# Attention scores computed once, in query rows, with the exponentials transposed afterwards

## The chip, the cores and the metric

The kernel runs on one core of a Trainium2 chip. The metric is the device time of one execution in microseconds (us). TensorE (PE) multiplies matrices, and its weight loads are listed apart (PEld); VectorE (DVE) and ScalarE (ACT) read and write both memories, PSUM and SBUF; GpSimd (POOL) works in SBUF alone; SyncE (SP) starts the transfers from and to DRAM. Each engine runs its own list of instructions in order and waits on semaphores. TensorE's granted clock is recorded as a share of 2.4 GHz: 1.00 is 2.4 GHz, 0.50 is 1.2 GHz, and what lies between is a mean over time at either level.

## What is computed

x has 8 batches of 112 queries with 256 features, the context 8 batches of 375 keys. Two layers follow one another; in each there is attention on the context and then a feed-forward part:

```python
x = x + _L0_xattn_ref(_layernorm(x), ctx, ...)       # 16 heads of 16, with biases, no mask
x = x + _L0_ffn_ref(_layernorm(x), ...)              # 8 experts, the best 2 for each token
x = x + _L1_xattn_ref(_layernorm(x), ctx, ..., mask) # 16 heads of 16, no biases, a 112 x 375 mask
x = x + _L1_ffn_ref(_layernorm(x), ...)              # rounded weights and a short convolution
```

The attention, in both layers:

```python
attn = jnp.einsum('bhqd,bhkd->bhqk', qp, kp) * SCALE
attn = jax.nn.softmax(attn, axis=-1)
out = jnp.einsum('bhqk,bhkd->bhqd', attn, vp)
```

The softmax goes over the 375 keys, so it needs a maximum over them for each query and head, exponentials, and their sum. The product with the values contracts over the keys, so the exponentials have to stand with the keys on the partitions for it. Products of full precision are made from a high and a low part of each operand (`product3`: high times high, high times low, low times high).

## The kernel before

The program has five stages: a setup (lines 82 to 108), attention a0, the experts, attention a1 (both from `attention_layer`), and the last feed-forward part. A barrier of all engines stands between stages. The setup loads x and waits for it before the barrier.

In `attention_layer` everything goes batch by batch, with the queries projected for all batches at the start. For one batch, in the order in which the data flow:

- `context` transposes the context (6 transposes into PSUM); ACT writes the high part, DVE the low part. `keys` and `values` project it: 12 matmuls of 376 columns and 18 of 256.
- `spread` copies the keys into a head layout `kst`. Each head pair has rows 0 to 47 and 64 to 111, with high and low parts stacked (48 = 3 x 16 rows), made by 16 matmuls with a selection matrix `sel` and 4 evictions of 752 columns. `stacked` does the same to the queries (`qst`), once for each half of the batches.
- `scores_for_max` computes the scores with the queries on the partitions (two heads to a matmul pair, L695), and `maxima` on DVE takes the maximum of each row (L469 in a0; in a1 the mask is added in the same instruction, L473).
- `parts`, `max_rows` (L703) and `shift` turn the maxima into rows and subtract them from the queries by two more rows of the contraction.
- `scores` computes the scores a second time, now with the keys on the partitions: six units a batch, each of 8 matmuls of 50 rows (L723). In a1 each unit has 4 more matmuls of 448 columns which add the mask (L717). ACT takes the exponential of each unit in one instruction of 896 columns (L343).
- `weigh` multiplies by the values: four groups a batch, each 12 matmuls that write 32 columns of the array (L738; each is recorded twice, so 24). A column of ones gives the sum. `gathered`, `turned` and `output` transpose back, DVE divides, and the output projection and the addition to x follow.

Two PSUM tiles `pair` of 1024 columns are handed around in the order of the list `order`, one tile `s1` holds the scores for the maxima, and `misc` holds the small products in the order of `small`. A unit in a tile waits until the reader of the unit before in the same tile is done. The loop over b interleaves the second scores of batch b, the first scores of b+1, and the context of b+2; the order of the calls in the tensor block is the order on TensorE. GpSimd does nothing in the loop.

## Time and profile before

| | |
|---|---|
| median of 3 runs | 889.59 us (885.14 to 893.82) |
| the profiled execution | 894.33 us, span 892.6 us |
| setup and attention a0 | 0 to 267.7 us of the span |
| first exponential of a0, of a1 | at 76.9 us, at 607.2 us |
| experts | 267.7 to 538.0 us |
| attention a1 | 538.0 to 804.5 us |
| last feed-forward part | 804.5 to 892.6 us |
| busy over the span | PE 669.3 us, DVE 434.3 us, ACT 288.7 us, POOL 47.5 us |

The stage borders are the first instructions after each barrier. Busy time of PE is the union of its matmuls from issue to modelled end, so a group of matmuls that is listed with 0.65 us gives the array to the next group earlier than that: what a group costs in a full row of work is the distance from its start to the start of the next one.

### The profile page before, as it was taken

Reading aid. Unit: us, or ns where it says so; the run is one execution under the profiler, and the core shown is the slowest. Engines: PE = TensorE matmul, PEld = TensorE weight load, DVE = VectorE, ACT = ScalarE, POOL = GpSimd, SP = SyncE. Lnnn points to the kernel's source line nnn. Section 1 sums busy time; section 2 is a strip of 40 time slices with the busy share of each in tenths; the row PEclk is TensorE's granted clock in tenths of the full one; section 3 lists DMA queues with packets and bytes.
Section 4 is the critical chain, followed back from the end, with each engine's and each line's share of the span. In section 5 each row is a group of like instructions: output and inputs, shape, how many; then the busy total and the mean of one; then the engine's idle time right before and its main releaser. Section 6 shows DMA issues by size and latency. Waiting matters only on the chain. (4 is left out here: it accounts for less than half of the span.)

```text
span 892.6 us, 13908 instructions
## 1 busy us (share of the span) xinstructions
PE 669.3 (75%) x5473; PEld 552.5 (62%) x5473; DVE 434.3 (49%) x1204; ACT 288.7 (32%) x505; POOL 47.5 (5%) x59
## 2 busy tenths in 40 slices
PE   0679989898883604999998722879999999982744
PEld 0657777777662604998898721767777777762533
DVE  3556555656613240243221344465555546626895
ACT  1433343444322001332233212324433343334530
POOL 1010000000000042000000071000000000000000
PEclk9988778999756655999999965989999999995888
DMA  5000000000009844455555023000000000000001
GB/s 141 23 17 18 19 11 9 1 1 1 1 2 302 258 182 158 174 179 175 178 177 171 25 82 112 13 18 19 19 19 1 1 1 1 2 2 1 1 0 41
DMA packets 39728, 57.05 MB, mean 64 GB/s; under 512 B 5209, under 2 KB 32881, under 8 KB 39537
## 3 DMA queue, kind: packets, MB, share of 16 engines
q1 hardware_dynamic: 38128, 52.50, 18.3%
q0 software_dynamic: 1536, 3.67, 1.3%
q8 instruction: 44, 0.72, 0.3%
q14 instruction: 20, 0.16, 0.1%
HBM read 47.91 MB, written 8.26 MB: 63 GB/s over the span
## 5 line engine op out<-in xcount | busy, mean ns | idle before, releaser
L343 ACT ACTIVATE a_e<-a_pair 125x896 f32<-125x896 f32 x96 | 88.2, 919 | 145.0 <-PE a_pair L723 143.8
L473 DVE CUSTOM_DVE_ANT_0 a_masked<-a_s,a_mask 112x375 f32<-112x375 f32 x128 | 65.3, 544 | 52.2 <-issue 52.2
L1385 PE MATMUL ex_h<-ex_xg_t,w_s 128*128 128x128 f32 x672 | 80.8, 280 | 0.1
L1133 ACT ACTIVATE ex_h_t<-ex_h,b_e 128x128 f32<-128x128 f32 x168 | 47.9, 369 | 101.4 <-PE ex_h L1385 101.4
L1385 PEld LDWEIGHTS ex_h<-ex_xg_t,w_s 128*128 128x128 f32 x672 | 79.0, 197 | 0.5 <-DVE ex_xg_t L1280 0.5
L1397 PE MATMUL ex_y<-w_s,ex_h_t 128*128 128x256 f32 x336 | 75.8, 379 | 0.0
L469 DVE TENSOR_REDUCE a_mx<-a_s 112x2 f32<-112x750 f32 x64 | 59.9, 936 | 29.2 <-PE a_s L695 28.6
L723 PEld LDWEIGHTS a_pair<-a_q,a_kst 50*125 50x125 f32 x768 | 55.1, 203 | 27.3 <-issue 20.4
L723 PE MATMUL a_pair<-a_q,a_kst 50*125 50x112 f32 x768 | 67.1, 298 | 4.3 <-DVE a_kst L463 4.2
L695 PE MATMUL a_s<-a_kst,a_qst 48*112 48x376 f32 x256 | 54.8, 422 | 19.2 <-DVE a_mx L469 10.8
L1397 PEld LDWEIGHTS ex_y<-w_s,ex_h_t 128*128 128x128 f32 x336 | 62.3, 190 | 7.6
L670 PE MATMUL a_pair<-a_kp,a_sel 128*128 128x376 f32 x256 | 58.3, 352 | 0.9 <-ACT a_kst L327 0.8
L39 PE MATMUL a_pair<-a_ct,a_wr 128*128 128x376 f32 x192 | 48.7, 418 | 12.7 <-DVE a_ct L444 12.7
L1286 DVE TENSOR_TENSOR ex_y_sb<-ex_y,b_all 128x256 f32<-128x256 f32 x21 | 8.9, 425 | 100.2 <-PE ex_y L1397 100.2
L738 PE MATMUL a_av<-a_e,a_v 125*32 125x112 f32 x1536 | 57.4, 293 | 0.0
L717 PE MATMUL a_pair<-ident_r,a_mask_r 112*125 112x448 f32 x192 | 50.5, 384 | 4.6 <-DVE a_kst L463 4.2
L39 PEld LDWEIGHTS a_pair<-a_ct,a_wr 128*128 128x128 f32 x192 | 43.3, 248 | 14.5 <-issue 11.5
L738 PEld LDWEIGHTS a_av<-a_e,a_v 125*32 125x32 f32 x1536 | 41.0, 122 | 12.1 <-issue 10.6
L670 PEld LDWEIGHTS a_pair<-a_kp,a_sel 128*128 128x128 f32 x256 | 41.9, 190 | 7.8 <-issue 6.3
L695 PEld LDWEIGHTS a_s<-a_kst,a_qst 48*112 48x112 f32 x256 | 24.8, 185 | 31.5 <-issue 13.0
L39 PE MATMUL a_misc<-a_wr,a_ct 128*125 128x256 f32 x288 | 42.8, 294 | 1.8 <-ACT a_v L337 1.6
L39 PEld LDWEIGHTS a_misc<-a_wr,a_ct 128*125 128x125 f32 x288 | 36.8, 189 | 7.6 <-issue 7.6
(252 smaller groups left out, 917.4 us busy)
## 6 DMA issues: line engine op xcount, KB each, us to landing
w_s<-in_L_ffn_W SPq DMA_DIRECT2D x21, 1024.0 KB, 5.0
w_all<-in_L_ffn_W SPq DMA_DIRECT2D x8, 1024.0 KB, 12.0
a_ctx<-in_ctx SPq DMA_DIRECT2D x16, 375.0 KB
x_slots<-ex_zeros SPq DMA_DIRECT2D x1, 2688.0 KB, 13.5
ex_xg<-x_slots SPq DMA_DIRECT2D x21, 128.0 KB, 4.8
y_slots<-ex_y_sb SPq DMA_DIRECT2D x21, 128.0 KB, 1.7
b_all<-in_L_ffn_b SPq DMA_DIRECT2D x1, 1024.0 KB
wu<-in_L_ffn_w SPq DMA_DIRECT2D x1, 1024.0 KB, 5.9
```

The costliest lines, as they stand in the source:

```text
L39: ins = nc.tensor.matmul(out, a, b, start=first and k == 0 and n == 0, stop=last and k == len(w) - 1 and n == 2)
L343: a.activation(es[:, c, kc], halves(bank("s2", b, c, kc)[0:KP], 4 * S), ACT.Exp, scale=scale)\
L469: v.reduce_max(mx[:, t], halves(s1[0:S], SK), AX.X).then_inc(max_out, 1)
L473: ins = v.tensor_tensor_reduce(out=masked[:, e], in0=s1[0:S, e * 512:e * 512 + SK], in1=mask_sb[:], scale=1.0, scalar=-3.0e38, op0=ALU.add ...
L670: last = nc.tensor.matmul(bank("ks", b, i)[:, j * 512:j * 512 + SKP], sel[:, 1, part, n], kp[:, part, c], start=part == 0, stop=part == 1)
L695: last = nc.tensor.matmul(s1[0:S, e * 512:e * 512 + SKP], qst[rows, t, columns(b)], kst[rows, b % 3, t], start=True, stop=True)
L717: nc.tensor.matmul(out[0:KP, e * 512:e * 512 + 4 * S], mask_r[:, part, ks], ident_r[0:S, :], start=part == 0, stop=False)
L723: last = nc.tensor.matmul(out[0:KP, e * 512 + n * S:e * 512 + (n + 1) * S], kst[rows, b % 3, t, ks], q2[rows, t], start=mask is None, stop ...
L738: last = nc.tensor.matmul(av[32 * n:32 * n + 32, g * S:(g + 1) * S], vx[:, b % 3, kc, 2 * (4 * c + n) + e], es[:, c, kc, e, n * S:(n + 1) ...
L1133: last = a.activation(h_t[:, i % 2, f], hb[i % 2][:, f * 128:(f + 1) * 128], ACT.Gelu, bias=b1_e[:, i % 2, f:f + 1])
L1385: last = nc.tensor.matmul(hb[i % 2][:, f * 128:(f + 1) * 128], w1_s[:, i % 3, k, f * 128:(f + 1) * 128], xg_t[:, i % 2, k * 128:(k + 1) * ...
L1397: last = nc.tensor.matmul(yb[i % 2][:, 0:D], h_t[:, i % 2, f], w2_s[:, i % 2, f * D:(f + 1) * D], start=f == 0, stop=f == FC - 1)
```

## The change

- The scores are computed once, with the queries on the partitions. A step t covers four heads of one batch (32 steps in a layer). Its 12 matmuls of 376 columns work on 32 rows each, rows 32r to 32r+31 for head r, in three passes (high times high, high times low, low times high); the four heads write four PSUM banks of the one tile `s`. The queries for even and odd heads lie in `qz` with the other head's rows set to zero, so that the keys need no layout of their own: `kst`, `qst`, `sel`, `spread`, `stacked`, `parts`, `max_rows`, the second scores and the mask matmuls go.
- `maxima` takes two heads at a time and then scales the two maxima into the bias of the exponential. `exps` makes one ACTIVATE for each head (112 x 375). In a0 it reads PSUM; in a1 it reads the masked scores, which the maximum instruction now writes to SBUF.
- `turned` transposes the exponentials: three PSUM units a step, each of 4 transposes, copied to `et`: one by ACT and two by DVE in a0, two by ACT and one by DVE in a1.
- PSUM is now `s` (4 banks) and a ring of four single banks in the order of `order`.
- The high and low parts of context, keys and attention output (from batch 1 on for context and keys) are made by GpSimd, two instructions each, from a raw copy that ACT takes out of PSUM. GpSimd also adds the output bias batch by batch, and computes the reciprocal deviation with a power.
- The setup no longer loads x: a0 loads it in two halves among its weights. Biases are loaded as rows and turned by small matmuls. The second half of the queries is normalized, transposed and projected in steps 0 to 4 of the loop.

The core of the diff, indentation reduced; of functions that are rewritten only the new lines stand:

```diff
-    @block.sync
-    def _(sp):
-        sp.dma_start(x_sb[:], x.rearrange("b s d -> s b d")).then_inc(x_in, 16)
-        sp.wait_ge(x_in, 16)
...
     wr = sb(f"{tag}_wr", [128, 2, 4, DC, D], F32R)
-    qst = sb(f"{tag}_qst", [128, HP, T], F32R)
-    kst = sb(f"{tag}_kst", [128, 3, HP, SKP], F32R)
...
+    kp = sb(f"{tag}_kp", [128, 2, 2, DC, SKP], F32R)
...
-    vx = sb(f"{tag}_v", [KP, 3, KC, H, 32])
-    mx = sb(f"{tag}_mx", [S, HP, 2])
...
+    s = pb(f"{tag}_s", (128, 2048))
+    ring = [pb(f"{tag}_ring{i}") for i in range(4)]
...
+    order = [("wt", 1), ("wt", 0)] if transposed else [("bias",)]
+    order += [("ct", 0, 0), ("ct", 0, 1), ("k", 0, 0), ("k", 0, 1), ("xt", 0, 0), ("xt", 0, 1), ("q", 0, 0), ("q", 0, 1)]
+    order += [("wt", 2), ("wt", 3)] if transposed else [("bo",)]
+    order += [("v", 0, 0), ("v", 0, 1)]
+    for t in range(-1, NQ + 4):
+        b, g = divmod(t, 4)
+        step = [("et", t, kc) for kc in range(KC)] + [("av", t - 1)]
+        step = [u for u in step if 0 <= u[1] < NQ]
+        work = [[("v", b + 1, 0)], [("avt", b - 1), ("k", b + 1, 0)], [("ot", b - 1), ("v", b + 1, 1), ("k", b + 1, 1)],
+                [("ct", b + 2, 0), ("ct", b + 2, 1), ("y", b - 1)]][g]
+        order += step + [u for u in work if 0 <= u[1] < B]
+        order += {2: [("xt", 1, 0), ("xt", 1, 1)], 3: [("q", 1, 0)], 4: [("q", 1, 1)]}.get(t, [])
     place = {u: i for i, u in enumerate(order)}
...
+            def load_x(half):
+                bs = slice(4 * half, 4 * half + 4)
+                sp.dma_start(x_sb[:, bs], x_from.rearrange("b s d -> s b d")[:, bs]).then_inc(x_in[half], 16)
+
+            if x_from is not None:
+                load_x(0)
+                sp.dma_start(b_row[:, 0:D], bias_q.rearrange("(o n) -> o n", o=1)).then_inc(b_in, 16)
+                sp.dma_start(b_row[:, D:3 * D], bias_kv.rearrange("(o n) -> o n", o=1)).then_inc(b_in, 16)
+            sp.dma_start(w_raw[:, 1], sources[1]).then_inc(w_in[1], 16)
+            load_ctx(0)
+            sp.dma_start(w_raw[:, 0], sources[0]).then_inc(w_in[0], 16)
...
+            def context(b, c):
+                wait_read(pool, "ct", b, c)
+                wait_filled(pool, "k", b - 1, 1)
+                wait_filled(pool, "v", b - 1, 1)
+                g_.tensor_copy(ct[:, 0, c, 0:SK], ct_raw[:, c]).then_inc(ct_hi, 1)
+                pool.wait_ge(ct_hi, 2 * (b - 1) + c + 1)
+                g_.tensor_tensor(ct[:, 1, c, 0:SK], ct_raw[:, c], ct[:, 0, c, 0:SK].bitcast(F32),
+                                 ALU.subtract).then_inc(ct_lo, 1)
+
+            def keys(b, m):
+                wait_read(pool, "k", b, m)
+                if b >= 2:
+                    pool.wait_ge(s_filled, 4 * (b - 1))
+                g_.tensor_copy(kp[:, b % 2, 0, m], k_raw[:, m]).then_inc(k_hi, 1)
+                pool.wait_ge(k_hi, 2 * (b - 1) + m + 1)
+                g_.tensor_tensor(kp[:, b % 2, 1, m], k_raw[:, m], kp[:, b % 2, 0, m].bitcast(F32),
+                                 ALU.subtract).then_inc(k_lo, 1)
+
...
+            for t in range(-1, NQ + 4):
+                b, g = divmod(t, 4)
+                if t == 0:
+                    deviation(1)
+                if g == 1:
+                    if b + 1 < B:
+                        keys(b + 1, 0)
+                    if b >= 1 and mask is None:
+                        biased(b - 1)
+                if g == 2:
+                    if b >= 1:
+                        output(b - 1)
+                    if b + 1 < B:
+                        keys(b + 1, 1)
+                if g == 3 and b + 2 < B:
+                    context(b + 2, 0)
+                    context(b + 2, 1)
 
...
+            def exps(t, i):
+                act.wait_ge(max_out, 2 * t + i + 1)
+                if mask is None and t >= 2:
+                    wait_filled(act, "et", t - 2, 2)
+                for r in (2 * i, 2 * i + 1):
+                    src = s[0:S, r * 512:r * 512 + SK] if mask is None else es[:, t % 2, r, 0:SK]
+                    last = a.activation(es[:, t % 2, r, 0:SK], src, ACT.Exp, bias=shift[:, t % 2, r:r + 1],
+                                        scale=scale)
+                last.then_inc(e_out, 1)
+
+            def turned(t, kc):
+                wait_filled(act, "et", t, kc)
+                if t >= 2:
+                    wait_filled(act, "av", t - 2)
+                a.activation(et[:, t % 2, kc], bank("et", t, kc)[0:KP, 0:4 * S], ACT.Copy)\
+                    .then_inc(is_read("et", t, kc), 1)
...
+            for t in range(-1, NQ + 4):
+                b, g = divmod(t, 4)
+                if 0 <= t < NQ:
+                    turned(t, 0)
+                if t + 1 < NQ:
+                    exps(t + 1, 0)
+                if 0 <= t < NQ and mask is not None:
+                    turned(t, 2)
+                if t + 1 < NQ:
+                    exps(t + 1, 1)
+                if 0 <= t - 1 < NQ:
+                    weighed(t - 1)
+                if g == 0 and b + 1 < B:
+                    values(b + 1, 0)
+                if g == 1 and b + 1 < B:
+                    keys(b + 1, 0)
+                if g == 2:
+                    if b >= 1:
+                        output(b - 1)
+                    if b + 1 < B:
+                        values(b + 1, 1)
+                        keys(b + 1, 1)
+                if g == 3 and b + 2 < B:
+                    context(b + 2, 0)
+                    context(b + 2, 1)
+                if t == 2:
+                    normal(1, 0)
...
+            def maxima(t, i):
+                dve.wait_ge(s_filled, t + 1)
+                pair = slice(2 * i, 2 * i + 2)
+                if mask is None:
+                    v.reduce_max(mx[:, t % 2, pair], s[0:S].rearrange("p (r n) -> p r n", r=4)[:, pair, 0:SK],
+                                 AX.X).then_inc(max_raw, 1)
+                else:
+                    if t >= 2:
+                        wait_filled(dve, "et", t - 2, 2)
+                    for r in (2 * i, 2 * i + 1):
+                        v.memset(tick[:, r % 2:r % 2 + 1], 0.0)
                         ins = v.tensor_tensor_reduce(
...
+            for t in range(-1, NQ + 4):
+                b, g = divmod(t, 4)
+                if t + 1 < NQ:
+                    maxima(t + 1, 0)
+                    maxima(t + 1, 1)
+                if 0 <= t < NQ:
+                    turned(t, 1)
+                    if mask is None:
+                        turned(t, 2)
+                if g == 1 and b >= 1:
+                    divided(b - 1)
+                if g == 3 and b >= 1:
                     add(b - 1)
...
+            def scores(t):
+                b, g = divmod(t, 4)
+                c, e = divmod(g, 2)
+                at = 2 * (DC * (b // 4) + c) + 2
+                pe.wait_ge(qz_odd if e else qz_even, at)
+                if b:
+                    pe.wait_ge(k_lo, 2 * (b - 1) + c + 1)
+                else:
+                    wait_read(pe, "k", 0, c)
+                if t:
+                    pe.wait_ge(e_out if mask is None else max_out, 2 * t)
+                for n, (i, j) in enumerate(((0, 0), (0, 1), (1, 0))):
+                    for r in range(4):
+                        rows = slice(32 * r, 32 * r + 32)
+                        last = nc.tensor.matmul(s[0:S, r * 512:r * 512 + SKP], qz[rows, e, i, c, columns(b)],
+                                                kp[rows, b % 2, j, c], start=n == 0, stop=n == 2)
+                last.then_inc(s_filled, 1)
+
+            def turned(t, kc):
                 if kc == 0:
...
-            def scores_for_max(b, t):
-                if t % 2 == 0:
-                    wait_read(pe, "ks", b, t // 2)
-                if HP * b + t:
-                    pe.wait_ge(max_out, HP * b + t)
-                for e in range(2):
-                    rows = slice(64 * e, 64 * e + NS)
-                    last = nc.tensor.matmul(s1[0:S, e * 512:e * 512 + SKP], qst[rows, t, columns(b)],
-                                            kst[rows, b % 3, t], start=True, stop=True)
-                last.then_inc(s1_filled, 1)
...
+            for t in range(-1, NQ + 4):
+                b, g = divmod(t, 4)
+                if t + 1 < NQ:
+                    scores(t + 1)
+                if 0 <= t < NQ:
+                    for kc in range(KC):
+                        turned(t, kc)
+                if 0 <= t - 1 < NQ:
+                    weigh(t - 1)
+                if g == 0 and b + 1 < B:
+                    values(b + 1, 0)
+                if g == 1:
+                    if b >= 1:
+                        gathered(b - 1)
+                    if b + 1 < B:
+                        keys(b + 1, 0)
+                if g == 2:
+                    if b >= 1:
+                        turned_o(b - 1)
+                    if b + 1 < B:
+                        values(b + 1, 1)
+                        keys(b + 1, 1)
+                if g == 3:
+                    if b + 2 < B:
+                        context(b + 2, 0)
+                        context(b + 2, 1)
+                    if b >= 1:
+                        output(b - 1)
+                if t == 2:
+                    turned_x(1, 0)
+                    turned_x(1, 1)
+                if t == 3:
+                    queries(1, 0)
+                if t == 4:
+                    queries(1, 1)
             end_phase()
```

## Rows read from the trace of the kernel before

**Rows 1.** Busy time by stage; columns: length, busy us of each engine (x instructions), granted clock, DMA.
```profile
0.00:267.70 267.70, 211.94 (x1932) 170.38 (x1932) 139.59 (x259) 100.00 (x139) 8.77 (x16) 0.85 0.07 20
538.00:804.50 266.50, 228.56 (x2136) 178.63 (x2136) 143.03 (x562) 97.33 (x127) 3.28 (x7) 0.94 0.06 17
...
76.90:265.00 188.10, 167.96 (x1717) 135.17 (x1718) 100.93 (x184) 76.81 (x106) 0.00 (x0) 0.82 0.03 8
```
**Rows 2.** Timeline of DVE, additions of batches 1, 4 (a0) and 1, 4 (a1); start, length.
```profile
151.97 0.42 DVE L515 TENSOR_TENSOR x_sb<-x_sb,a_misc 112x256 f32<-112x256 f32 x1 [1.57 <-PE a_misc L39]
...
222.49 0.42 DVE L515 TENSOR_TENSOR x_sb<-x_sb,a_misc 112x256 f32<-112x256 f32 x1 [1.60 <-PE a_misc L39]
...
680.32 0.42 DVE L515 TENSOR_TENSOR x_sb<-x_sb,a_misc 112x256 f32<-112x256 f32 x1 [1.40 <-PE a_misc L39]
...
761.70 0.42 DVE L515 TENSOR_TENSOR x_sb<-x_sb,a_misc 112x256 f32<-112x256 f32 x1 [1.35 <-PE a_misc L39]
```
**Rows 3.** Timeline of PE in a1, no idle time between the groups.
```profile
715.92 0.78 PE L738 MATMUL a_av<-a_e,a_v 125*32 125x112 f32 x24
716.63 0.66 PE L703 MATMUL a_pair<-ident_r,a_mparts 112*128 112x112 f32 x4
717.13 1.04 PE L717 MATMUL a_pair<-ident_r,a_mask_r 112*125 112x448 f32 x4
718.10 0.64 PE L723 MATMUL a_pair<-a_q,a_kst 50*125 50x112 f32 x8
718.58 0.38 PE L695 MATMUL a_s<-a_kst,a_qst 48*112 48x376 f32 x2
718.89 0.65 PE L748 MATMUL a_misc<-ident,a_avs 128*112 128x128 f32 x4
719.30 2.29 PE L39 MATMUL a_pair<-a_ct,a_wr 128*128 128x376 f32 x12
721.43 0.97 PE L717 MATMUL a_pair<-ident_r,a_mask_r 112*125 112x448 f32 x4
```
**Rows 4.** Groups by shape on DVE, ACT and POOL; busy us, mean ns, idle before.
```profile
L343 ACT ACTIVATE a_e<-a_pair 125x896 f32<-125x896 f32 x96 | 88.2, 919 | 145.0 <-PE a_pair L723 143.8 <-DVE a_qst L596 1.2
L473 DVE CUSTOM_DVE_ANT_0 a_masked<-a_s,a_mask 112x375 f32<-112x375 f32 x128 | 65.3, 544 | 52.2 <-issue 52.2
L469 DVE TENSOR_REDUCE a_mx<-a_s 112x2 f32<-112x750 f32 x64 | 59.9, 936 | 29.2 <-PE a_s L695 28.6
...
L489 DVE TENSOR_TENSOR a_q<-a_qst,a_pair 128x448 fp32r<-128x448 f32 x32 | 19.7, 616 | 15.0 <-PE a_pair L703 15.0
...
L350 ACT ACTIVATE a_avs<-a_av 128x448 f32<-128x448 f32 x16 | 8.7, 544 | 8.4 <-PE a_av L738 8.0
L320 ACT ACTIVATE a_kp<-a_pair,a_bk 128x376 fp32r<-128x376 f32 x16 | 8.3, 571 | 29.4 <-PE a_pair L39 29.4
...
L481 DVE CAST a_mparts<-a_mx 112x8 fp32r<-112x8 f32 x32 | 5.6, 176 | 1.1
...
L301 POOL TENSOR_TENSOR x_sb<-x_sb,a_bo_all 112x2048 f32<-112x2048 f32 x1 | 4.6, 4632 | 32.8 <-DVE a_bo_all L577 32.8
...
L297 POOL CAST a_sel<-ident 128x128 fp32r<-128x128 f32 x12 | 3.0, 292 | 0.1
```
**Rows 5.** Timeline of a0: its first matmuls, and the eviction that begins its tail.
```profile
15.82 1.49 PE L649 MATMUL a_pair<-ident,a_ctx 125*128 125x125 f32 x6 [15.82 <-DMA a_ctx<-in_ctx]
...
261.00 0.55 ACT L350 ACTIVATE a_avs<-a_av 128x448 f32<-128x448 f32 x1 [4.17 <-PE a_av L738]
```
**Rows 6.** Busy time by stretch, columns as in rows 1: attention without mask, with mask, transposes alone.
```profile
240.00:256.00 16.00, 14.89 (x159) 11.78 (x158) 4.51 (x12) 5.46 (x8) 0.00 (x0) 0.50 0.01 2
784.00:796.00 12.00, 12.00 (x154) 9.38 (x154) 2.33 (x11) 5.57 (x8) 0.00 (x0) 1.00 0.01 2
...
513.40:517.00 3.60, 3.53 (x16) 3.16 (x16) 3.53 (x3) 1.02 (x1) 2.99 (x3) 0.53 0.20 59
517.00:519.00 2.00, 1.91 (x16) 1.71 (x16) 0.98 (x3) 1.82 (x2) 1.70 (x2) 1.00 0.20 63
```

More of the change, by code:

```diff
@@ L21 @@
 HALF = T // 2
-HP = H // 2
-NS = 3 * DH
-NSM = NS + 2
 E, F = 8, 1024
@@ L223, in attention_layer @@
[L223 to L231 removed]
+                NQ = 4 * B
@@ new lines, in _ @@
+                        act.wait_ge(filled, 3)
+                        context(0, 0)
+                        context(0, 1)
+                        if not transposed:
+                            weight(1, 0)
+                            wait_read(act, "bias")
+                        keys(0, 0)
+                        keys(0, 1)
+                        normal(0, 0)
+                        normal(0, 1)
+                        if not transposed:
+                            weight(2, 2)
+                            weight(3, 3)
@@ L376, in _ @@
+                        queries(0, 0)
+                        odd_heads(0, 0)
+                        queries(0, 1)
+                        odd_heads(0, 1)
+                        if transposed:
+                            weight(2, 2)
+                            weight(3, 3)
                         values(0, 0)
                         values(0, 1)
[L378 to L383 removed]
@@ new lines, in _ @@
+                        first_keys(0)
+                        first_keys(1)
+                        turned_x(0, 0)
+                        turned_x(0, 1)
+                        if not transposed:
+                            weight(2, 2)
+                            weight(3, 3)
+                        dve.wait_ge(side_out, 1)
+                        for m in range(DC):
+                            queries(0, m)
+                            even_heads(0, m)
+                        if transposed:
+                            weight(2, 2)
+                            weight(3, 3)
+                        else:
+                            dve.wait_ge(bo_in, 16)
+                            wait_filled(dve, "bo")
+                            v.tensor_tensor(bo_all[:], bo[:], bank("bo")[0:S, 0:D], ALU.add).then_inc(is_read("bo"), 1)
@@ new lines, in out_bias @@
+                        def out_bias():
+                            wait_read(pe, "bias")
+                            pe.wait_ge(w_in[3], 16)
+                            wait_free(pe, "bo")
+                            for c in range(DC):
+                                last = nc.tensor.matmul(bank("bo")[0:S, 0:D], bvb[:, c * S:(c + 1) * S], w_raw[:, 3, c],
+                                                        start=c == 0, stop=c == 1)
+                            last.then_inc(is_filled("bo"), 1)
@@ L798, in _ @@
-                        if mask is None:
-                            pe.wait_ge(bv_out, DC)
-                            pe.wait_ge(w_in[3], 16)
-                            wait_seat("bo")
-                            for c in range(DC):
-                                last = nc.tensor.matmul(misc[0:S, 0:D], bvb[:, c], w_raw[:, 3, c], start=c == 0, stop=c == 1)
-                            last.then_inc(misc_filled, 1)
-                        if transposed:
-                            wait_read(pe, "wt", 1)
-                        else:
-                            pe.wait_ge(w_lo, 4)
```

1001 lines of the change are left out of this document (396 added, 605 removed).

## Prediction

> **What bounds the kernel now.** I read the busy time by stage first. The two attention stages take 267.7 and 266.5 of the 892.6 us [rows 1], and the diff touches nothing else. In the loop of a0 TensorE is busy 168 of 188 us, VectorE 101, ScalarE 77, GpSimd not at all [rows 1]: TensorE is the resource. Its clock is a mean 0.82 there, so about 36% of that time ran at 1.2 GHz ((1 - 0.82) / 0.5).
>
> The additions to x then give the period of a batch: (222.49 - 151.97) / 3 = 23.5 us in a0 and (761.70 - 680.32) / 3 = 27.1 us in a1 [rows 2].
>
> The timeline of PE in a stretch without idle time prices each kind of work at the full clock, from one start to the next [rows 3]: `weigh` 0.71 us a group, `max_rows` 0.50, a mask unit 0.97, a second-score unit 0.48, a first-score pair 0.31, four transposes 0.41 (0.10 each), twelve matmuls of 376 columns 2.13 (0.178 each; 0.12 for 256 columns). A batch adds up to: context 0.6, keys 2.1, values 2.2, spread 16 x 0.178 = 2.8, first scores 8 x 0.31 = 2.5, maxima rows 1.0, second scores 6 x 0.48 = 2.9, weigh 2.8, the tail of the batch 0.4 + 0.2 + 0.7 = 1.3. That is 18.2 us, and 24.0 in a1 with 6 x 0.97 of mask. The rest of the periods is slow clock in a0 and small waits.
>
> **What goes and what comes on TensorE.** Out: 2.8 + 2.5 + 1.0 + 2.9 = 9.2 us a batch, in a1 15.0. In: 48 transposes at 0.10, 4.9 us, and four times twelve score matmuls of 32 rows. The trace shows no matmuls in four row groups. Below, three passes that run four abreast cost 3 x 0.178 = 0.53 us a step; above, twelve in file cost 2.1. The nearest row is the pair on rows 0 to 47 and 64 to 111: it takes 0.31, only 0.13 more than one [rows 3]. I take 0.53 + 0.13 = 0.67, so 2.7 a batch. The new sum is 9.0 + 4.9 + 2.7 = 16.6 us a batch or 4.2 a step, in both layers. TensorE alone would then give 32 x 4.2 = 134 us a layer.
>
> **The new chain in a0.** `s` is one buffer. `scores(t+1)` waits until all exponentials of t have read it, and everything of PE's next step stands behind that wait. The loop is: scores 0.67; the result is there 0.07 to 0.24 after the array is free (0.38 against 0.31, 0.65 against 0.41 [rows 3]), say 0.15; twice a maximum over 750 columns 0.94 [rows 4] and the scaling, priced as the small cast at 0.18, with 0.05 between, 2.3; two exponentials. One costs 0.57: the ACT copy with a bias operand of the same width [rows 4]. With 0.1 for hand-overs the loop takes 0.82 + 2.3 + 1.14 + 0.1 = 4.4 us. It is longer than PE's 4.2, so PE waits.
>
> It waits more in three steps of four. DVE copies its two transposed units only after both maxima, at 0.62 each (the 448-column eviction [rows 4]), so their banks come free 3.7 and 4.4 us after the scores began, and the ring gives these banks to the late work. The PE is through scores, transposes and weigh at 0.67 + 1.23 + 0.71 = 2.6. In g = 1 the keys wait until 3.7 and end at 4.8; in g = 2 values and keys end at 5.5; in g = 3 the second context half and the projection end at 5.1. In g = 0 the values wait for GpSimd's parts of the context: a subtraction of 375 columns is 4.63 / 2048 x 375 = 0.85 us and a cast 0.25 / 128 x 375 = 0.73 (3.0 us for 12 [rows 4]), so two halves take 3.4 us with their own waits, from ACT's raw copy at 5.2. They are done at 8.6, 3.5 into the next step, and the values end at 4.9. Together 4.4 x 4 + 0.4 + 1.1 + 0.7 + 0.5 = 20.3, a step of 5.1 us. The keys' parts by GpSimd have two steps to spare and cost nothing; GpSimd as a whole has some 9 us of work in 20.
>
> **The new chain in a1.** The masked scores go to SBUF, so `s` is free after the maxima: 0.82 + 2 x (2 x 0.54 + 0.23) = 3.4 us, no bound. ScalarE is: four exponentials 2.3, two copies 1.1 (0.54 each [rows 4]), the eviction of 112 columns 0.26 (by the line through 448 and 896 columns, 0.17 + 0.84 per thousand), raw copies 3.3 a batch or 0.8: 4.45 us a step. PE has 4.2 and waits on the exponentials before its transposes. I add 0.55, somewhat less than in a0: 5.0 us. DVE has about 3.6 and is not late.
>
> **Prologue.** In a0 the first matmul waits for the context at 15.8 [rows 5], and the first exponential comes at 76.9 (the border of the second stretch in [rows 1]), because first scores of a whole batch, the head layouts and the next batch stand ahead of it. Now: stage begins 4 us earlier without the load of x, but half of x goes ahead of the context, so context at 12.5; transposes 1.5 (as now, [rows 5]) and parts, 15.2; keys at the slow rate 3.9; x 1.6; parts 1.3; queries 3.5; the parts, the zeroed copies and the values behind them 3. First scores at 28.5. SP's two bias loads cost issue time only, covered by the transfer of x. In a1, counted from 538.0, weights are transposed first and nothing of x is loaded; the same terms give 24.6. The second half of the queries (about 14 DVE instructions of up to 0.62, at steps 0 to 4, part of it in slack) costs 6 us a layer.
>
> **Tail.** From the last `gathered` eviction to the end of the stage are 267.7 - 261.0 = 6.7 us now [rows 1, 5]; the last transposes, weigh and GpSimd's two parts of the output come on top: 10, and the barrier 1.3.
>
> **The sum.** a0: 28.5 + 32 x 5.1 + 6 + 10 + 1.3 = 209 against 267.7, -59. a1: 24.6 + 32 x 5.0 + 6 + 10 + 1.3 = 202 against 266.5, -64. Together -123 at the full clock.
>
> **The clock.** In 16 us of a0 without keys, values and masks the clock was 0.50 though PE was busy 14.9; in the same part of a1, with mask matmuls of 448 columns, 1.00 [rows 6]. The change takes the mask out of a1 and puts wide scores and many transposes in. I take a slow share of 15%, between a1's 0 and a0's 36%. In a slow stretch a step needs 2 x 4.2 = 8.4 us for 5.05, so a share s costs 323 / (1 - 0.4 s) - 323: 21 us at 0.15, 54 at 0.36. The forecast on the profiled execution is 894.3 - 123 + 21 = 792; the median of the runs lies 4.7 below that execution, so 788.
>
> **Rivals.**
> *The clock stays low.* Transposes are 4.9 of 16.6 us of PE work; if they do not hold the clock up, and waits of up to 1 us a step pull it down, both layers run mostly at 1.2 GHz. At a share of 0.8 the cost is 152: 894.3 - 123 + 152 - 4.7 = 918 us, slower. It decides from a share of 0.69 on, where the 123 are used up. For it: the 0.50 in rows 6. Against it: in the 3.6 us from 513.4 PE did nothing but 128-column transposes at a clock of 0.53, and the next 2 us, transposes too, ran at 1.00 [rows 6]. The Trainium skill, "TensorE: Matmul & The Clock Gate", Part 4, says of transposes that the full clock "doesn't engage for transpose-mode"; by that rule this rival would be the likeliest. The trace does not agree with it. 6%.
> *Row groups run in file.* Scores cost 2.1 instead of 0.67, on a0's chain in full, in a1 on PE's sum (5.6). About +45 in each layer less some cover, 788 + 85 = 873. Against it: the pair at 0.31. 6%.
> *GpSimd is late.* If its parts take twice as long beside DVE, the context parts are done 3.4 us later, for 6 batches and 2 layers +41, with some of the keys' output: 835. The only GpSimd rows of this size come from quiet stretches. 10%.
> *Little of the waiting comes.* Steps of 4.5 and a full clock: 788 - 21 - 64 x 0.55 = 732. 16%.
> The change could also not do what it says only in that the one buffer `s` lets nothing overlap; that is inside the chain above.
>
> **How the numbers follow.** The forecast has 62%, 755 to 830. The range, 738 to 850, takes in the GpSimd case, the 36% share (788 + 33 = 821) with it, and most of the quick case; it leaves out the two dear rivals and the ends. 1% is what a measurement can tell from no change, 881 to 898. Slower by more than that is the clock rival and a mixture of it with rows in file, 7%; within 1% 3%; faster 90%.
>
> **What would show it.** In the profile after: distance between score groups (L of `scores`) 5.1 us in a0 and 5.0 in a1; a score group's start to the next PE group 0.6 to 0.7, against 2.1 for the second rival; the first exponential near 31 us, and near 565 less what a0 saves; granted clock by stretch in both loops; PE waiting before keys and values on DVE's copies, and before `values` in g = 0 on GpSimd. I am wrong if the step is above 6.5 us in either layer, or if the prologue of either layer takes more than 35 us.

## The result and the profile after

| | before | after |
|---|---|---|
| median of the runs | 891.71 us | 780.81 us |
| the runs (4 each) | 885.14 to 905.89 | 776.57 to 781.32 |
| profiled execution, span | 894.3, 892.6 | 776.57, 774.5 |

The ratio is 0.8766, 95% interval 0.8718 to 0.8815: faster, near the forecast of 788. It leaves out the execution before of 905.89 us, which fell in a slower state of the chip; without it the median before is 889.59 us. The path to the number was less good: a cost of 21 us did not come, TensorE had more work than the sum gave it, and it waited less.

Busy time by stage comes first (columns as in [rows 1]): a0, experts, a1, the last stage, then the steady part of both loops.

```profile
0.00:208.30 208.30, 171.95 (x1976) 140.16 (x1976) 138.38 (x272) 126.40 (x272) 59.15 (x94) 0.97 0.09 26
208.30:478.30 270.00, 188.88 (x1193) 170.40 (x1193) 86.88 (x240) 60.60 (x187) 36.41 (x40) 0.82 0.52 170
478.30:686.50 208.20, 168.91 (x1976) 138.13 (x1976) 123.23 (x554) 138.12 (x304) 52.21 (x77) 0.94 0.07 22
686.50:774.50 88.00, 42.02 (x212) 33.76 (x212) 65.03 (x145) 31.21 (x54) 0.00 (x0) 0.75 0.05 11
49.40:197.00 147.60, 132.08 (x1651) 106.14 (x1650) 106.87 (x196) 99.87 (x217) 47.01 (x69) 1.00 0.03 10
520.00:679.00 159.00, 141.18 (x1786) 114.53 (x1775) 100.96 (x472) 119.05 (x266) 44.80 (x66) 1.00 0.03 9
```

a0 takes 208.4 us against 267.7, a1 208.7 against 266.5 (from 477.9, where its first loads are issued, to 686.6). The last two rows hold the surprise: the granted clock is 1.00 through the steady part of both loops. In a0 it was 0.82 in the long loop of [rows 1]; in a1 it had been 1.00 before, too (607 to 800 us).

The additions to x again give the period (timeline of VectorE; a0 batches 1 and 4, then a1):

```profile
101.19 0.42 DVE L605 TENSOR_TENSOR x_sb<-x_sb,a_ring 112x256 f32<-112x256 f32 x1 [1.10 <-PE a_ring L36]
...
164.59 0.42 DVE L605 TENSOR_TENSOR x_sb<-x_sb,a_ring 112x256 f32<-112x256 f32 x1 [1.12 <-PE a_ring L36]
...
580.49 0.42 DVE L605 TENSOR_TENSOR x_sb<-x_sb,a_ring 112x256 f32<-112x256 f32 x1 [1.40 <-PE a_ring L36]
...
643.96 0.42 DVE L605 TENSOR_TENSOR x_sb<-x_sb,a_ring 112x256 f32<-112x256 f32 x1 [1.39 <-PE a_ring L36]
```

That is 63.40 / 3 = 21.13 and 63.47 / 3 = 21.16 us a batch, 5.28 us a step, against 23.5 and 27.1 [rows 2]. One steady batch on TensorE, the work of g = 0, 1, 2, 3 in turn:

```profile
101.08 0.78 PE L779 MATMUL a_s<-a_kp,a_qz 32*112 32x376 f32 x12
101.79 1.56 PE L788 MATMUL a_ring<-ident,a_e 112*125 112x112 f32 x12
103.28 0.78 PE L802 MATMUL a_ring<-a_et,a_v 125*32 125x112 f32 x24
103.99 1.69 PE L36 MATMUL a_ring<-a_wr,a_ct 128*125 128x256 f32 x12
105.91 0.77 PE L779 MATMUL a_s<-a_kp,a_qz 32*112 32x376 f32 x12 [0.23 <-ACT a_e L411]
...
109.59 1.26 PE L36 MATMUL a_ring<-a_ct,a_wr 128*128 128x376 f32 x6
110.78 0.77 PE L779 MATMUL a_s<-a_kp,a_qz 32*112 32x376 f32 x12
...
114.84 0.95 PE L36 MATMUL a_ring<-a_wr,a_ct 128*125 128x256 f32 x6 [0.74 <-DVE a_et L589]
115.63 1.21 PE L36 MATMUL a_ring<-a_ct,a_wr 128*128 128x376 f32 x6
116.77 0.78 PE L779 MATMUL a_s<-a_kp,a_qz 32*112 32x376 f32 x12
...
120.84 0.51 PE L721 MATMUL a_ring<-ident,a_ctx 125*128 125x125 f32 x3 [0.62 <-DVE a_et L589]
121.37 0.93 PE L36 MATMUL a_ring<-a_wr,a_ot 128*112 128x256 f32 x6
122.23 0.77 PE L779 MATMUL a_s<-a_kp,a_qz 32*112 32x376 f32 x12
```

Twelve score matmuls hold TensorE for 101.79 - 101.08 = 0.71 us, the transposes for 1.49, the weighing for 0.71. The waits are the three in brackets: for the exponentials at g = 0, and at g = 2 and 3 for a bank that VectorE's copy (L589) frees. The first lies in the step whose scaling took 0.77 us instead of 0.17 (below): there the chain is 4.8 us long.

Groups by shape show the operations on the chain and beside it (columns as in [rows 4]):

```profile
L411 ACT ACTIVATE a_e<-a_s,a_shift 112x375 f32<-112x375 f32 x128 | 66.4, 571 | 12.5 <-DVE a_shift L582 12.2
L570 DVE TENSOR_REDUCE a_mx<-a_s 112x2 f32<-112x750 f32 x64 | 59.7, 933 | 32.7 <-PE a_s L779 32.7
L582 DVE TENSOR_SCALAR a_shift<-a_mx 112x2 f32<-112x2 f32 x128 | 33.9, 265 | 4.4
L276 POOL TENSOR_TENSOR a_ct<-a_ct_raw,a_ct 128x375 fp32r<-128x375 f32 x28 | 25.8, 920 | 2.2
```

The exponential (0.57) and the maximum (0.94) were priced right. The scaling L582, a few elements, was priced 0.18 and has a mean of 0.265.

### The profile page after: what moved, and what is told of

Read it like the earlier page. It is cut to its first block and busy times, and to the rows that moved or that the text cites. A ratio compares the mean times of both kernels' runs of the same rounds, so it can differ in the third digit from the quotient of the medians.

```text
span 774.5 us, 14634 instructions
## 1 busy us (share of the span) xinstructions
PE 571.8 (74%) x5357; PEld 482.4 (62%) x5357; DVE 413.5 (53%) x1210; ACT 356.3 (46%) x816; POOL 147.8 (19%) x210
## 5 line engine op out<-in xcount | busy, mean ns | idle before, releaser
L788 PE MATMUL a_ring<-ident,a_e 112*125 112x112 f32 x768 | 102.2, 284 | 3.0 <-ACT a_e L411 3.0
L788 PEld LDWEIGHTS a_ring<-ident,a_e 112*125 112x125 f32 x768 | 90.7, 192 | 19.9 <-issue 14.8
L577 DVE CUSTOM_DVE_ANT_0 a_e<-a_s,a_mask 112x375 f32<-112x375 f32 x128 | 65.2, 542 | 39.3 <-issue 21.9
L419 ACT ACTIVATE a_et<-a_ring 125x448 f32<-125x448 f32 x96 | 51.5, 536 | 53.1 <-PE a_ring L788 53.1
L411 ACT ACTIVATE a_e<-a_e,a_shift 112x375 f32<-112x375 f32 x128 | 70.4, 599 | 11.9 <-DVE a_shift L582 11.1
L411 ACT ACTIVATE a_e<-a_s,a_shift 112x375 f32<-112x375 f32 x128 | 66.4, 571 | 12.5 <-DVE a_shift L582 12.2
L589 DVE COPY a_et<-a_ring 125x448 f32<-125x448 f32 x96 | 56.9, 621 | 3.5 <-PE a_ring L788 3.3
L779 PE MATMUL a_s<-a_kp,a_qz 32*112 32x376 f32 x768 | 50.7, 365 | 8.5 <-ACT a_e L411 6.4
L36 PE MATMUL a_ring<-a_wr,a_ct 128*125 128x256 f32 x288 | 44.2, 302 | 14.0 <-DVE a_et L589 9.0
L36 PEld LDWEIGHTS a_ring<-a_wr,a_ct 128*125 128x125 f32 x288 | 38.2, 197 | 19.7 <-issue 12.7
L802 PE MATMUL a_ring<-a_et,a_v 125*32 125x112 f32 x1536 | 50.1, 263 | 0.0
L779 PEld LDWEIGHTS a_s<-a_kp,a_qz 32*112 32x112 f32 x768 | 29.7, 173 | 21.5 <-issue 18.8
```

What stands on the lines that cost most here:

```text
L36: ins = nc.tensor.matmul(out, a, b, start=first and k == 0 and n == 0, stop=last and k == len(w) - 1 and n == 2)
L411: last = a.activation(es[:, t % 2, r, 0:SK], src, ACT.Exp, bias=shift[:, t % 2, r:r + 1], scale=scale)
L419: a.activation(et[:, t % 2, kc], bank("et", t, kc)[0:KP, 0:4 * S], ACT.Copy)\
L577: ins = v.tensor_tensor_reduce(out=es[:, t % 2, r, 0:SK], in0=s[0:S, r * 512:r * 512 + SK], in1=mask_sb[:], scale=1.0, scalar=-3.0e38, op0 ...
L589: v.tensor_copy(et[:, t % 2, kc], bank("et", t, kc)[0:KP, 0:4 * S]).then_inc(is_read("et", t, kc), 1)
L779: last = nc.tensor.matmul(s[0:S, r * 512:r * 512 + SKP], qz[rows, e, i, c, columns(b)], kp[rows, b % 2, j, c], start=n == 0, stop=n == 2)
```

## The experiments

Stages not touched (the experts above all) vary by a few us from run to run, so each kernel's steady periods stand beside its time. Medians are of four runs (five for the minimum, two for one row group). "To before" is the ratio to the kernel before, run again beside each set, with its 95% interval; periods are from the additions three batches apart, as above.

| kernel | median us | to before | a0, a1 us a batch |
|---|---|---|---|
| after | 780.81 | 0.8766 (0.8718 to 0.8815) | 21.13, 21.16 |
| groups in file | 780.65 | 0.8767 (0.8696 to 0.8838) | 21.16, 21.21 |
| one row group | 877.58 | 0.9825 (0.9726 to 0.9923) | 26.18, 27.29 |
| single products | 743.33 | 0.8309 (0.8228 to 0.8391) | 18.75, 18.26 |
| copy early | 772.37 | 0.8693 (0.8626 to 0.8760) | 20.73, 20.07 |
| one input | 772.20 | 0.8674 (0.8592 to 0.8757) | 20.65, 20.67 |
| no GpSimd parts | 781.05 | 0.8802 (0.8731 to 0.8874) | 20.90, 21.20 |
| minimum | 758.09 | 0.8471 (0.8389 to 0.8554) | 18.93, 20.21 |
| scores first | 770.21 | 0.8640 (0.8546 to 0.8735) | 21.13, 21.16 |
| all three | 752.03 | 0.8405 (0.8322 to 0.8488) | 19.35, 19.46 |
| best | 743.23 | 0.8318 (0.8253 to 0.8382) | 18.95, 19.47 |
| single pass everywhere | 738.66 (one run) | | 18.03, 17.90 |
| one group, single products | 869.23 (one run) | | irregular |

**Do the four row groups run side by side?** First the order was changed:

```diff
-for n, (i, j) in enumerate(((0, 0), (0, 1), (1, 0))):
-    for r in range(4):
+for r in range(4):
+    for n, (i, j) in enumerate(((0, 0), (0, 1), (1, 0))):
```

> The same 12 score matmuls, but all three of one head (one row group) before the next head's, so that neighbours on TensorE are mostly of one row group. Theory: the four groups run side by side only when neighbours differ, and TensorE is what bounds the step (19.4 of 21.1 us busy per batch in the kernel after). Then the group of scores goes from 0.70 us towards the 12 x 0.178 = 2.1 us of the prediction's second case, and the program from 781 to about 781 + 64 x 1.4 = 870 us (850 to 885). Rival 1: the order does not matter to the overlap: 0.70 us again and 781 us. Rival 2: the overlap is lost but TensorE had slack beside the exponentials: under 64 x 0.7, so below 825 us.

The theory fell, as rival 1 had it: 780.65 us, and the group takes 101.42 - 100.69 = 0.73 us. The overlap does not need a different group at every turn. Then all were put into one group, so that three heads of four get the scores of the first:

```diff
-rows = slice(32 * r, 32 * r + 32)
+rows = slice(0, 32)
```

> All 12 score matmuls of a step read rows 0 to 31, so they share one row group (heads of the other groups get the first group's scores; the output differs). Theory: it is the four different row groups that let 12 matmuls end in 0.70 us, whatever their order; in one group they take 12 x 0.178 = 2.1 us, and since TensorE is what bounds, the program rises by 64 x 1.4 = 90 us to 870 us (855 to 885), above 85% of what the change had won. Rival: narrow matmuls overlap in one group too, or are shorter than 0.178 us: group of scores under 1.3 us, program under 820 us.

877.58 us, inside the theory's range. PE's timeline:

```profile
144.05 2.30 PE L779 MATMUL a_s<-a_kp,a_qz 32*112 32x376 f32 x12
146.28 1.56 PE L788 MATMUL a_ring<-ident,a_e 112*125 112x112 f32 x12
```

2.23 us against 0.71: without the row groups 97 of the 109 us that the change won (889.59 - 780.81) are gone. It is also what the second rival (873 us) would have looked like.

**What bounds a step?** Products off the chain were cut to one pass of three; the results lose their low parts.

```diff
-return product3(nc, out, w, x)
+for k, ((wh, wl), (xh, xl)) in enumerate(zip(w, x)):
+    ins = nc.tensor.matmul(out, wh, xh, start=k == 0, stop=k == len(w) - 1)
+return ins
```

> The products by context, keys, values, queries and outputs make one of their three passes; scores, transposes, the weighing and all waits stay. Per batch TensorE loses about two thirds of 6 us (keys 2.4, values 2.6, output 0.9), 3.9 us, none of it on the chain from scores to exponentials. Theory 1 (TensorE's own work bounds the step): a batch falls from 21.1 to 17.5 to 18.5 us, where the first layer's chain of 4.4 to 4.6 us a step takes over; 14 steady batches give 40 to 50 us, and the program is at 730 us (720 to 742). Theory 2 (the chain and the bank waits bound it): a batch stays above 20.5 us and the program above 770 us. Clock: transposes are then the largest share of TensorE's work. If only matmuls with operands other than an identity hold the clock, windows of both loops fall below 1.00; if any work does, they stay at 1.00.

The batches fell by 2.4 and 2.9 us, of 3.9 taken out. 743 us is 1 us above the first theory's range and far below the second's; a0's 18.75 us lies above the 17.5 to 18.5 that the first gave a batch, a1's 18.26 inside. So TensorE's own work is most of the bound. At 18.3 to 18.8 it waits again: in three batches of a0 4.3 us for banks that VectorE's copies free and 1.7 us for exponentials. The next kernel takes the bank waits away:

```diff
 maxima(t + 1, 0)
-maxima(t + 1, 1)
 turned(t, 1)
+maxima(t + 1, 1)
 if mask is None: turned(t, 2)
```

> VectorE makes the second of its three blocks of turned exponentials between its two pairs of maxima instead of behind both, in both layers. Theory (bank stalls): TensorE's 1.7 us of idle time per batch before context transposes, values and keys end on that copy; they go, and a batch takes 19.7 to 20.4 us instead of 21.1. In the first layer the chain from scores to exponentials grows by the copy's 0.62 us to about 5.0 to 5.2 us and may just take over. Program 770 us (762 to 782), the gain mainly in the second layer, whose scores wait for the maxima alone. Rival (the chain bounds the first layer already): first layer 208 + 32 x 0.6 = 227 us, program about 795 us.

The median lies inside the range of the theory. a1, whose chain has room, gained 1.1 us a batch; a0 gained 0.4 and was not lengthened, so the rival fell. But a0's 20.73 us a batch is above the 19.7 to 20.4 of the theory: the waits for VectorE's copies did not go there, 3.5 us in three batches are left of 4.0.

**The scaling beside GpSimd.** The timeline of after shows what draws the scaling out. The second view is of the kernel with one-input operations (the next experiment), where L276 is a cast:

```profile
102.77 0.85 POOL L276 TENSOR_TENSOR a_ct<-a_ct_raw,a_ct 128x375 fp32r<-128x375 f32 x1
102.88 0.77 DVE L582 TENSOR_SCALAR a_shift<-a_mx 112x2 f32<-112x2 f32 x1
...
112.11 0.98 POOL L285 TENSOR_TENSOR a_kp<-a_k_raw,a_kp 128x376 fp32r<-128x376 f32 x1
112.58 0.54 DVE L582 TENSOR_SCALAR a_shift<-a_mx 112x2 f32<-112x2 f32 x1
```

```profile
557.67 0.50 POOL L276 CAST a_ct<-a_ct_raw 128x375 fp32r<-128x375 f32 x1
557.89 0.31 DVE L580 TENSOR_SCALAR a_shift<-a_mx 112x2 f32<-112x2 f32 x1
...
110.42 0.73 POOL L297 TENSOR_TENSOR x_sb<-x_sb,a_bo_all 112x256 f32<-112x256 f32 x1
110.45 0.72 DVE L580 TENSOR_SCALAR a_shift<-a_mx 112x2 f32<-112x2 f32 x1
```

Each drawn-out scaling ends within 0.05 us of the end of a GpSimd operation (103.65 and 103.62; 113.12 and 113.09; 558.20 and 558.17; 111.17 and 111.15), and the third of these is a cast with one input. That experiment made `g_.tensor_tensor(..., ALU.subtract)` into `g_.tensor_copy(...)` in the parts of context, keys and outputs, so that a second high part stands where the low part should be.

> GpSimd's subtractions (two inputs) for context, keys and outputs become copies (one input), as many, so the low parts are not computed. Theory: the scaling of a pair of maxima on VectorE (169 ns at best, mean 265 ns, up to 772 ns) is drawn out only beside GpSimd's two-input operations; its mean falls to about 175 ns. Since it lies on the chain from scores to exponentials and TensorE is busy 92% of a step, only part of the 12 us returns: 776 us (770 to 781). Rival 1: the chain bounds the step, and all 12 us return: 769 us. Rival 2: the scaling is drawn out by any GpSimd work: mean stays about 260 ns, 781 us.

772.20 us, at the low side of the theory's range; the mean of the scaling fell to 208 ns, neither the theory's 175 nor rival 2's 260. Of the 128 scalings 14 are still drawn out (39 in after): seven beside the addition of the bias (L297, two inputs), seven beside casts, to between 0.22 and 0.46 us. So the theory that only two-input operations do it is refuted. After has the same: five scalings of a1 take 0.30 to 0.33 us, to the end of a cast (L274). What the runs show is that a scaling that begins beside a GpSimd operation nearly always lasts until the end of it; the casts are shorter (0.50 us against 0.85 to 1.00), and fewer scalings meet one. The scalings are 7 us shorter in all, and GpSimd's parts are shorter, too; together 0.5 us a batch came back in either layer, and the two are not told apart here. Next the parts of context and keys left GpSimd, which kept those of the outputs and the bias:

```diff
-a.activation(ct_raw[:, c], bank("ct", b, c)[:, 0:SK], ACT.Copy)     # then GpSimd: cast, subtract
+a.activation(ct[:, 0, c, 0:SK], bank("ct", b, c)[:, 0:SK], ACT.Copy)
+v.tensor_tensor(ct[:, 1, c, 0:SK], bank("ct", b, c)[:, 0:SK], ct[:, 0, c, 0:SK].bitcast(F32), ALU.subtract)
```

(and the keys in the same way.)

> The parts of context and keys of every batch are made as for the first: the high part by ScalarE from the bank, the low part by VectorE from the same bank, nothing of it by GpSimd. VectorE gets four subtractions of some 0.5 us more per batch: 15.1 + 2.2 = 17.3 of 21.1 us in the first layer. Theory: TensorE stays the bound, the banks of the keys and contexts come free one VectorE operation later, and the scaling is drawn out less often: 785 us (775 to 798). Rival 1: GpSimd's share was what made the layers short, since VectorE's queue delays the maxima by each subtraction: 64 x 0.5 = 32 us, 813 us. Rival 2: the parts were better on VectorE all along, the interference with GpSimd (12 us) was the larger cost: 770 us.

781.05 us, inside the theory's range and no different from after. The scaling's mean fell to 171 ns (one of the 128 is drawn out), a0 gained 0.2 us a batch, a1 nothing. "Parts by GpSimd" is the part of the change that brought nothing. In three batches of a0 the subtractions take VectorE 7.2 us, and its scalings 4.1 us where they took 8.1 in after: more than half of what GpSimd takes off VectorE comes back as longer scalings.

Last, the scaling itself was taken out. The factor is a power of two, so multiplying the queries by it loses nothing, and the sign goes in with it:

```diff
+v.tensor_scalar(side[:], side_raw[:], -scale, None, ALU.mult)
-v.reduce_max(mx[:, t % 2, pair], ...)
-v.tensor_scalar(shift[:, t % 2, pair], mx[:, t % 2, pair], -scale, None, ALU.mult)
+v.tensor_reduce(shift[:, t % 2, pair], ..., AX.X, ALU.min)
-a.activation(..., ACT.Exp, bias=shift[...], scale=scale)
+a.activation(..., ACT.Exp, bias=shift[...], scale=-1.0)
```

> The queries are multiplied by minus the score factor when heads are split, a minimum over the negated scores is the exponentials' offset, and the scaling of each pair of maxima (128 operations, 33.9 us, mean 265 ns) is gone; the mask is multiplied once. The chain loses two scalings, and VectorE's copies of turned exponentials come 0.35 to 0.9 us earlier. Theory (TensorE's work of 19.4 us per batch bounds, the rest is bank waits): the waits of 1.7 us per batch shrink to about 0.8, a batch takes 20.3 us, program 767 us (760 to 773). Rival 1 (the chain bounds): two scalings with their gaps, 0.6 us, on 64 steps: 743 us. Rival 2: the bank waits have another cause: 779 us.

758 us, 2 us below the theory's range; the first rival (743 us) is not reached. Three batches of a0, then two of a1, from the busy times:

```profile
97.35:154.13 56.78, 56.73 (x724) 46.83 (x728) 37.26 (x58) 39.98 (x93) 22.46 (x34) 1.00 0.03 9
590.67:631.10 40.43, 38.40 (x484) 31.22 (x488) 23.63 (x110) 30.87 (x71) 13.59 (x20) 1.00 0.01 2
```

In a0 TensorE is busy 56.73 of 56.78 us. So a batch of its work is 18.9 us, below the 19.2 to 19.4 that I had taken from its busy time in after, and nothing but work is left.

**The start of the second layer.** In after, TensorE waits for the query weights, and the context's transposes stand behind that wait in its order; the values stand ahead of the first scores:

```profile
486.25 1.11 PE L686 MATMUL a_ring<-ident,a_w_raw 128*128 128x128 f32 x4 [4.51 <-DMA a_w_raw<-in_L_xattn_Wq]
...
503.99 3.64 PE L36 MATMUL a_ring<-a_wr,a_ct 128*125 128x256 f32 x18 [3.00 <-DVE a_wr L527]
507.56 1.01 PE L779 MATMUL a_s<-a_kp,a_qz 32*112 32x376 f32 x12
```

```diff
+if transposed: act.dma_start(w_raw[:, 0], sources[0]).then_inc(w_in[0], 16)    # in place of sp.dma_start
+scores(0)
 wait_weight(2, 2)
 values(0, 0)
```

> Second layer: the query weights are loaded by ScalarE's queue beside SyncE's loads. Both layers: TensorE makes the first group of scores before the first batch's values, not behind them. Theory: TensorE no longer waits 4.5 us for the query weights, and the 3.6 us of values lie beside the first maxima: first scores of the second layer at 22 to 24 us from its start instead of 29.7, loop ends 5 us earlier; first layer 1 to 3 us earlier; program 774 us (768 to 778). Rival: the first steps are bound by TensorE's backlog (values, keys, second half of the queries), so that what is won before the first scores is waited off behind it: 780 us.

770.21 us, inside the range, at its low side:

```profile
484.21 1.51 PE L724 MATMUL a_ring<-ident,a_ctx 125*128 125x125 f32 x6 [2.37 <-DMA a_ctx<-in_ctx]
...
497.27 0.77 PE L782 MATMUL a_s<-a_kp,a_qz 32*112 32x376 f32 x12
```

The stage begins at 476.5 there, so the first scores come at 20.8 us instead of 29.7. The first step then takes 7.4 us instead of 3.75, which gives 3.6 of the 8.9 back (the rival's mechanism), and the last addition comes 5.0 us earlier in the stage; in a0 3.1.

**Together.**

> The early copy, the scores first with the query weights on ScalarE's queue, and the minimum in place of maximum and scaling, together. Theory: a batch cannot go below TensorE's 19.2 to 19.4 us; first layer 19.9, second 19.6 us per batch, 21.1 before, so 14 x 1.35 = 19 us, and 6 us ahead of the loops: 756 us (748 to 764). Rival: the three cures share the same waits, and the best of them is all there is: 767 us.

752.03 us, inside the theory's range. But a0's batch is 19.35, longer than the 18.93 with the minimum alone. TensorE is idle for 1.1 us in three of these batches, 0.7 of them in waits for VectorE's last copy of a step: with the minimum alone there was nothing left for the early copy to save, and it seems to delay what stands behind it. The edit was taken out of a0:

```diff
 maxima(t + 1, 0)
+if mask is not None: turned(t, 1)
 maxima(t + 1, 1)
+if mask is None: turned(t, 1); turned(t, 2)
```

> The minimum in place of maximum and scaling and the scores first in both layers, the early copy in the second layer alone. Theory: the early copy costs the first layer 19.35 - 18.92 = 0.43 us a batch where TensorE has no wait left, and gains the second layer 20.2 - 19.5 = 0.7: against all three everywhere 7 x 0.43 = 3 us less, 749 us (744 to 753). Rival: the difference of the two first layers is one of their first steps: 752 us.

743.23 us (742.07 to 743.48), below the range. The first layer gained the expected 0.40 us a batch; that is 3 us; by the profiled executions the second layer's first scores come 10.6 us earlier than with all three, of which the a0 stage makes 5.7, so nearly all of the rest lies in the stage of the experts, which no edit touches. Not all of the 9 us is the edit's. It is the best version, 0.8318 of the kernel before. What still waits in a1 is GpSimd's context parts:

```profile
PE a_ring L36 <- POOL a_ct L280: 2.3, 3, 0.8
```

(three batches, 551.99 to 610.39: us in total, times, longest; the only wait of PE there.)

**The clock.** Two kernels were run for the granted clock alone.

> Scores too make one of their three passes (4 matmuls for 12), beside the single passes of keys, values, queries and output, so that in the loops transposes and the weighing are some two thirds of TensorE's work, and the low parts are not used. Clock: if any work holds it, the steady part of both loops stays at 1.00; if the share of ordinary matmuls with long rows is what holds it, it falls below 0.9 there. Time if the clock holds: the first layer's chain loses 0.45 us a step (4.2 to 3.8), second layer bound by ScalarE: 730 us (720 to 740).

```profile
92.00:146.10 54.10, 45.26 (x556) 34.14 (x556) 45.89 (x82) 42.10 (x94) 22.29 (x34) 1.00 0.03 9
554.02:607.71 53.69, 43.79 (x556) 33.72 (x556) 42.48 (x190) 46.07 (x106) 20.23 (x30) 1.00 0.03 9
```

1.00 in three steady batches of each layer, though TensorE is idle for a sixth of them or more and about half of its work is transposes (in a0 the groups of e, context and outputs have 25 us, and all groups 48, overlaps counted twice). The time, 738.66 us, is inside the range for a clock that holds (720 to 740).

> Scores in one row group (12 matmuls of 32 rows in file, 2.24 us a step in the run that did only this) and single passes for keys, values, queries and output; the output differs. Question: which work lets the granted clock fall in a loop where TensorE is nearly always busy. Theory 1 (matmuls on few rows, alone in the array, do not hold it): they are now 9 of some 22 us a batch against 9 of 26 before, wide products are nearly gone, and windows of a batch in the steady loops fall to 0.9 or less in both layers; a batch takes 23 us or more, program 810 to 850 us. Theory 2 (any busy TensorE holds it): both loops stay at 1.00; a batch takes 22.3 to 23 us, program 800 us. In the run with single products and four row groups the steady batches stood at 1.00.

```profile
120.00:160.00 40.00, 39.07 (x350) 32.95 (x350) 21.95 (x44) 22.36 (x49) 9.60 (x14) 0.85 0.01 1
...
560.00:600.00 40.00, 38.78 (x270) 33.25 (x270) 22.41 (x101) 25.33 (x54) 9.99 (x14) 0.76 0.06 19
680.00:720.00 40.00, 39.61 (x305) 33.38 (x297) 17.53 (x87) 21.98 (x50) 10.72 (x16) 0.76 0.01 2
```

The clock falls although TensorE is busy 97 to 99% of these stretches: 869 us, above the range, on the side of the first theory. The only difference from single products, at 1.00 in its steady batches, is that the 12 score matmuls lie in one row group instead of four. With one row group and full products (877.58 us) the clock fell in part: 1.00 in the steady batches of a0, but 0.94 in three of four in a1:

```profile
620.18:647.91 27.73, 26.60 (x241) 22.94 (x242) 12.77 (x63) 15.70 (x36) 6.79 (x11) 0.94 0.05 15
647.91:674.68 26.77, 25.24 (x241) 21.63 (x242) 12.70 (x64) 15.67 (x36) 6.78 (x10) 1.00 0.06 16
```

## Why the prediction was right, and where it was not

**The sum held where it was a sum of lengths.** The two layers fell by 534.2 - 417.1 = 117.1 us; the terms gave 123 before the clock. In a0: first scores at 27.9 (28.5 forecast), from there to the last scores 165.3 (31 x 5.1 + 6 = 164.1), from there to the end 15.2 (16.4). In a1: 29.7 (24.6), 163.6 (161), 15.4 (16.3). Inside the 165.3 two errors cancel: a steady step took 5.28 us and not 5.1, and all that is not steady added 1.5 us to that and not 6.

**The clock term was mis-sized: 21 us, measured none.** The step that failed was "between a1's 0 and a0's 36%". The slow share of both steady loops is 0; over the whole loops, first steps included, the clock was 0.98 and 0.99. I took a0's low clock for something that keys, values and mask matmuls have to lift. The runs show more than that. With single products and all scores in one row group a0's loop ran at 0.73 to 0.90 with TensorE nearly always busy; the same products with scores in four groups ran at 1.00. Wide products matter as well: with one row group and full products a0's steady batches stood at 1.00 and a1's at 0.94 to 1.00. The kernel before is full of narrow matmuls, on 48 and 50 rows, and the change takes them out; its a1, with mask products, stood at 1.00 [rows 6]. That this was the cause in the kernel before itself is argued from these runs and not shown on it; a version of it without its narrow products was not tried.

**The first rival (clock stays low) did not come.** Transposes did not hold the clock down. The Trainium skill, "TensorE: Matmul & The Clock Gate", Part 4, says the full clock "doesn't engage for transpose-mode"; the traces disagree, with 1.00 in loops where transposes are four tenths (after, 8 of 19 us a batch) to half (single pass everywhere) of the work.

**The step's length was right, its make-up was not.** I had 16.6 us of work and 3.7 of waits in a batch, 20.3; it is 18.9 and 2.2, 21.13. The transposes of the exponentials take 1.49 / 12 = 0.124 each, not the 0.10 that I read off the four of the attention output (L748) in [rows 3] (48 of them: +1.1); scores 2.8 against 2.7, keys 2 x 1.19 against 2.1, values 2.4 against 2.2; the remaining 0.6 is context (0.9 against 0.6) and the end of the batch (1.6 against 1.3). The shortfall could have been seen before: in three batches of a1 (680.32 to 761.70) TensorE was busy 76.55 us, 25.5 a batch, where the same prices add up to 24.0. The chain was 4.22 instead of 4.4, read where nothing else is left, in a0's last steps (184.73, 188.95, 193.18). So it did not bind in three steps of four: "longer than PE's 4.2, so PE waits" failed, and TensorE's 4.7 bound. In g = 0 it did bind, by 0.23 us, with the drawn-out scaling in it. The bank waits came where they were put, in g = 2 and 3 (0.74, 0.62, for 1.1 and 0.7); in g = 1 there was none, and the wait of g = 0 was not the one for GpSimd's context parts. By g the steps are 4.8, 4.9, 6.0, 5.5, where I had 4.9, 4.8, 5.5, 5.1.

**a1 was not bound by ScalarE.** I had 4.45 plus 0.55 of waits; ScalarE is busy 47.1 of 63.5 us, 3.9 a step, and TensorE's work is as in a0. The 5 us that its start took longer lie in the waits for the query weights to land (4.5 us) and of the values for the low part of their weights (3.0), both ahead of the first scores in PE's order.

**The scores' 0.67 was right** at 0.71, and the second rival was dead. **GpSimd late** did not come: PE waited 2.0 us on its context parts in the whole run; its subtraction of 375 columns takes 0.85 us as priced, or 0.98 to 1.00, and the cast 0.50 where I had 0.73. What GpSimd does cost lies elsewhere, in VectorE's scalings. **Little waiting** (732 us, steps of 4.5) did not come either; the best kernel comes near it with 743 us, and its a0 has no waits at 4.7 us a step.

Two errors cancel in the number: on the profiled execution the forecast of 792 was 15 us too high (21 of clock, less 6 of length), and the median lies 4 us above that execution where I took 5 below. That the forecast came within 7 us of the median is in part luck.

## What to carry to other kernels

Narrow contractions belong in different row groups: here twelve matmuls on 32 rows took 0.71 us instead of 2.23, in both orders tried, and the clock stayed at 1.00. A buffer's turn is worth as much as work: find which engine frees each bank last, and copy earlier only where the chain has room. A tiny operation between a reduction and its user may be foldable (sign and factor into the operands), and it is the one that suffers beside a busy GpSimd.

## What the runs showed of the hardware

- VectorE's scaling of 112x2 elements in SBUF takes 0.17 us, but when it begins beside a GpSimd operation it nearly always lasts until the end of that: 0.54 to 0.77 us beside those with two inputs, 0.31 beside a cast, in the lines shown. The maxima, which read PSUM, kept their 0.93.
- Four row groups overlap even when three matmuls of one group follow each other: 0.73 us for twelve.
- The granted clock was 0.76 to 0.85 in stretches with TensorE busy 97 to 99% (one row group, single products), and 1.00 with it busy 84% (single pass everywhere, four groups).
